# Third and fourth pass of a graph network: a quad's share of the fetching products moved ahead of the quad's own sums on TensorE

## The chip, the cores and the metric

The kernel runs on one core of one Trainium2 chip. The metric is the device time of one execution in microseconds (us), and of several executions the median. The core has a matrix engine (TensorE, PE in the profile, with PEld for its weight loads), a vector engine (VectorE, DVE), a scalar engine (ScalarE, ACT), GpSimd (POOL), and SyncE (SP), which here only issues transfers. GpSimd issues the gathers.

## The reference, cut to what matters

Four graph layers follow one another over 6250 nodes with 96 features and 106250 edges, which are sorted by target node. Each layer reads a row of a node table for each edge's source, and sums the rows (or takes their maximum) into the edge's target:

```
x = LN(x + attention layer(x))           # pass 1
x = LN(x + mean-and-max layer(x))        # pass 2, with a batch norm
# pass 3
msg = feat[src] * ci[src, None]
agg = segment_sum(msg, dst) * cj[:, None]
x = LN(x + (agg @ weight + bias))
# pass 4
msgs = (x @ W)[src] * edge_weight[:, None]
x = LN(x + LN(segment_sum(msgs, dst) + bias) * gamma + beta)
```

The change touches the sums `segment_sum` of passes 3 and 4 alone.

## The kernel before, in words

Edges are cut into tiles of 128, four tiles make a quad, four quads a group. There are 832 tiles and 208 quads in each of the four passes; `q` is the quad, `k = q % 4` its place in the ring of buffers.

**Gathers.** GpSimd runs through the quads (L630) and issues one indirect transfer for each tile of a quad, 128 rows of the node table into `rows[:, k, j]`. Before quad `q` it waits until the sums of quad `q - 4` are done, since these read the same buffer: `rows` is four quads deep.

**The sums of a quad.** VectorE writes `same` (L1348 in pass 3; L1696 in pass 4, times the edge's weight): a matrix of ones that says which of 128 target places an edge goes to. TensorE's `spread` (L728 through `window`) multiplies `rows` by `same`, four fp32 products that the profile counts as 8 matmuls. ScalarE adds the result to `acc` in its own `spread`: `part_sum` (L1028), a copy of 511 columns (L1030), one column with its carry (L1032). VectorE starts `same` of quad `q` when the sums of `q - 2` are done.

**Fetched tiles.** From quad 18 to quad 195 every third quad is picked (60 in each pass), and GpSimd gathers only three of its four tiles. The fourth comes from TensorE, out of a copy of the whole node table on the chip, split into three bf16 parts: 49 products of a one-hot matrix `found` with the table's 49 node tiles (L925), added up in `bank[0]`. They are cut into three pieces of 16, 16 and 17 products, which belong to the three quads ahead of the picked one: `piece(q)` gives the piece of quad `q`, and so every quad from 15 to 194 has one. VectorE's `find` writes the piece of `found` (L1588; ahead of a first piece also L1583), and after the third piece its `take` (L1595) adds the three parts of `bank[0]` up into `rows[:, k, 3]`. The order on VectorE within a quad is `same`, `take` if the quad is picked, `find`. TensorE's `spread` of a picked quad waits for `take`; its `fetch` waits for `find`.

**Side tiles.** In pass 3 the first 49 quads each carry one node tile more: ScalarE scales it into `x_two` (L1205), TensorE turns it (L950), ScalarE copies the result to `x_two_t` (L1209), TensorE multiplies it by `rhs_u` (L958), and ScalarE copies this to `xu` (L1215). ScalarE's order in a quad is L1205, L1209, then its `spread` with L1028, L1030 and L1032, then L1215:

```
wait(act, u_turned, q - 1)
act.activation(x_two[:, k % 2, :], tile_row(x_nodes, q), ACT.Identity, ...).then_inc(u_x, 1)
...
spread(q, k, acc, F, bank[2 + 2 * (k % 2)], part_sum, s2.agg_done, s2.held, s2.copied)
...
    wait(act, u_mm, q + 1)
    act.copy(tile_row(xu, q), bank[3][:, P:P + 2 * F]).then_inc(u_done, 1)
```

TensorE turns the tile of quad `q` only when `u_x` has counted `q + 1` and `u_done` has counted `q`. In pass 4 the first 49 quads also have a side tile, but on VectorE (L1705) and ScalarE (L1243) alone.

**The order on TensorE** within a quad of pass 3 is: turn (L950), [products of finished node tiles, L934, from quad 197 on], `spread`, product with `rhs_u` (L958), `fetch`. In pass 4 it is: [L934], `spread`, `fetch`. All engines take their instructions in the order of the program.

Of the kernel before, what the change touches and what calls it, by code (L numbers as in the profile page):

```python
# [38 lines left out]
def wait(eng, sem, value):  # L39
    if isinstance(value, int) and value <= 0:  # L40
        return
    if isinstance(sem, Signal):
        eng.wait_ge(sem.sem, value + sem.base)
    else:
        eng.wait_ge(sem, value)
# [27 lines left out]
def gnn_kernel(nc, N, E, dims, a):  # L73
# [18 lines left out]
    def tiles_of(c, n=NT):  # L92
        return range(c * CT, min(n, (c + 1) * CT))
# [8 lines left out]
    def ready(c):  # L102


        left = N - min(N, (c + 1) * CN)
        return -(-(E - left) // QE) - 1
# [11 lines left out]
    def piece(q):  # L118

        for m in range(EVERY):  # L120
            g = order_of.get(q + EVERY - m)
            if g is not None:
                return g, m
        return None
# [5 lines left out]
    def arrivals(n, q):  # L130

        return 16 * sum(gathers(m, p) for m in range(n + 1) for p in range(q % GQ, q + 1 if m == n else NQ, GQ))

    def ripe(slot, lag):

        return [c for c in range(NC) if ready(c) + lag == slot]

    ctx = ExitStack()
    with ctx:
# [114 lines left out]
        def exact(t, n=1):  # L254

            return near[:, t:t + n, :] if t < NEAR else far[:, t - NEAR:t - NEAR + n, :]
# [133 lines left out]
        def side_tile(q, kind):  # L390
            return kind and (not isinstance(q, int) or q < NT)

        def static(q):
            return isinstance(q, int)
# [275 lines left out]
        def _(pe):  # L670
# [47 lines left out]
            def group_offsets(i):  # L718

                _, at = nc.values_load_multi_w_load_instructions(offs[0:1, bass.ds(i * GQ * TQ, GQ * TQ)], engines=[pe.engine],  # L720
                                                                 min_val=0, max_val=QE - P, skip_runtime_bounds_check_because=NODES)
                return [at[k * TQ:(k + 1) * TQ] for k in range(GQ)]

            def window(out, nrow, at, left, right):

                for j in range(TQ):
                    here = bass.ds(at[j], P) if j else slice(0, P)
                    mm = pe.matmul(out[0:nrow, here], left(j), right(j), start=(j == 0), stop=(j == TQ - 1), skip_group_check=True)  # L728
                return mm
# [178 lines left out]
            def spread(s, q, i, k, at):  # L908

                wait(pe, s.same_done, q + 1)  # L910
                wait(pe, rows_in[k], arrivals(s.n, q))
                if q in order_of:
                    wait(pe, fetched, s.picks + order_of[q] + 1)
                wait(pe, s.copied, q - 1)
                window(bank[2 + 2 * (k % 2)], F, at, lambda j: rows[:, k, j, 0:F], lambda j: same[:, k % 2, j, :]).then_inc(s.agg_done.sem, 1)

            def fetch(s, q):

                at = piece(q)
                if at is None:  # L920
                    return
                g, m = at
                wait(pe, found_done, (s.picks + g) * EVERY + m + 1)
                for t in range(piece_of[m], piece_of[m + 1]):
                    mm = pe.matmul(bank[0][:, 0:PARTS * F], found[:, t, :], exact(t)[:, 0, :], start=(t == 0), stop=(t == NT - 1),  # L925
                                   skip_group_check=True)
                mm.then_inc(found_used.sem, 1)
# [3 lines left out]
            def products(c, nrow, rhs, freed, done):  # L931
                wait(pe, freed, c - 1)
                for m, t in enumerate(tiles_of(c)):
                    mm = pe.matmul(pair_of_banks[c % 2][m // 2][:, (m % 2) * 2 * F:(m % 2 + 1) * 2 * F], acc[0:nrow, t * P:(t + 1) * P],  # L934
                                   rhs[:], start=True, stop=True)
                mm.then_inc(done, 1)


            s2 = passes[2]
# [3 lines left out]
            def third_pass(i, kind):  # L943
                places = group_offsets(i)
                for k in range(GQ):
                    q = i * GQ + k
                    if side_tile(q, kind):
                        wait(pe, u_x, q + 1)
                        wait(pe, u_done, q)
                        pe.transpose(bank[3][0:F, 0:P], x_two[:, k % 2, :], ident[:]).then_inc(u_turned, 1)  # L950
                    if static(q):
                        for c in ripe(q, 1):
                            wait(pe, s2.copied, ready(c) + 1)
                            products(c, F, rhs_4, d_sum, d_mm)
                    spread(s2, q, i, k, places[k])
                    if side_tile(q, kind):
                        wait(pe, u_cols, q + 1)
                        pe.matmul(bank[3][:, P:P + 2 * F], x_two_t[:, k % 2, :], rhs_u[:], start=True, stop=True).then_inc(u_mm, 1)  # L958
                    fetch(s2, q)

            rolled(pe, third_pass, WITH_SIDE)
            for c in ripe(NQ, 1):
                wait(pe, s2.copied, ready(c) + 1)
# [3 lines left out]
            s3 = passes[3]  # L967
# [3 lines left out]
            def fourth_pass(i, kind):  # L971
                places = group_offsets(i)
                for k in range(GQ):
                    q = i * GQ + k
                    if static(q):
                        for c in ripe(q, 1):
                            wait(pe, s3.copied, ready(c) + 1)
                            products(c, F1, rhs_5, e_sum, e_mm)
                    spread(s3, q, i, k, places[k])
                    fetch(s3, q)  # L980

            rolled(pe, fourth_pass, PLAIN)
            for c in ripe(NQ, 1):
                wait(pe, s3.copied, ready(c) + 1)
# [794 lines left out]
```

## Time and profile before

| | |
|---|---|
| time, median of 3 runs (lowest, highest) | 4281.43 us (4277.96, 4282.35) |
| the profiled execution: its time, its span | 4278.2 us, 4276.2 us |
| busy: PE, DVE, ACT, POOL | 3037.4, 2905.5, 1377.3, 3094.2 us |
| pass 3, first to last gather issued | 2305.2 to 3268.8 us |
| pass 4, first to last gather issued | 3288.5 to 4254.8 us |
| mean granted clock of TensorE, as a share of full speed | 0.843 |

Busy time is summed over the span, so it says how full an engine is, not whether the others wait for it. In a timeline a row gives the start, the duration, the engine, the line, and in brackets how long the engine had been idle before it and what released it.

### The profile page before, as it was taken

To read this page: it belongs to the slowest core of one execution; us is meant where nothing else is said; L and a number is where in the kernel's file an instruction comes from. 1 tells how busy PE (TensorE), PEld (TensorE's weight loads), DVE (VectorE), ACT (ScalarE), POOL (GpSimd) and SP (SyncE) were. 2 spreads that over 40 slices of the span, in tenths; PEclk is the share of its full clock that TensorE was granted. 3 is DMA by queue.
4 is the path that set the end of the run, shared out by engine and by line. 5 is a ranking of instruction groups with operands and counts; after the bars stand their busy time and mean duration, and the time that the engine had idled before them with its cause. 6 is when DMAs were issued, how large, how long until landed. Compare 5 with 4: busy or idle time off the path is not lost.

```text
span 4276.2 us, 68563 instructions
## 1 busy us (share of the span) xinstructions
PE 3037.4 (71%) x20922; PEld 2603.9 (61%) x20922; DVE 2905.5 (68%) x5203; ACT 1377.3 (32%) x4318; POOL 3094.2 (72%) x3246
## 2 busy tenths in 40 slices
PE   7777777777666766676683787667775567776776
PEld 6677777777656666666662565555554455555555
DVE  4666666666676666666666566666665687777777
ACT  2222222222444444444454332222223222222223
POOL 5677777777277777777757777777776777777776
PEclk7777878777689888888895898999986699999997
DMA  7776776676443333333322222222222222222222
GB/s 216 202 188 178 188 187 182 182 188 179 105 121 100 100 98 100 100 100 98 100 74 62 49 45 45 45 45 45 45 44 67 55 45 44 45 45 46 44 45 56
DMA packets 363802, 417.49 MB, mean 98 GB/s; under 512 B 225184, under 2 KB 277011, under 8 KB 363357
## 3 DMA queue, kind: packets, MB, share of 16 engines
q0 software_dynamic: 129280, 239.67, 23.0%
q1 hardware_dynamic: 234173, 173.44, 15.2%
q8 instruction: 186, 3.05, 0.3%
q14 instruction: 163, 1.34, 0.1%
HBM read 393.05 MB, written 19.77 MB: 97 GB/s over the span
## 4 chain that ended last, share of the span: by engine, by line
POOL 61%; issue 21%; PE 8%; DMA 4%; DVE 3%; ACT 1%; SPq 1%; ACTq 0%; DVEq 0%; POOLq 0%
POOL rows L630 60%; PE bank L728 3%; DMA rows<-kv_table,src_idx 2%; DMA rows<-pair_table,src_idx 1%; PE bank L934 1%; POOL acc_max L657 1%; PE bank L825 1%; SPq L448 0%; PE bank L741 0%; PE bank L742 0%; PE bank L773 0%; PE bank L682 0%; DVE prod L1417 0%; DVE score L1419 0%; DVE prod L1415 0%
## 5 line engine op out<-in xcount | busy, mean ns | idle before, releaser
L728 PE MATMUL bank<-same,rows 128*96 128x128 f32 x4992 | 766.3, 304 | 364.8 <-issue 208.7
L630 POOL DMA_INDIRECT rows<-kv_table,src_idx x832 | 793.7, 954 | 314.1 <-issue 272.4
L630 POOL DMA_INDIRECT rows<-pair_table,src_idx x832 | 787.9, 947 | 311.5 <-issue 247.7
L728 PEld LDWEIGHTS bank<-same,rows 128*96 128x96 f32 x4992 | 658.7, 184 | 469.0 <-issue 407.8
L1030 ACT COPY acc<-bank 96x511 f32 (+1 forms) x832 | 480.1, 577 | 1365.8 <-PE bank L728 1364.6
L630 POOL DMA_INDIRECT rows<-h_table,src_idx x772 | 732.3, 949 | 253.7 <-issue 235.0
L630 POOL DMA_INDIRECT rows<-ci_table,src_idx x772 | 729.6, 945 | 243.3 <-issue 234.7
L1588 DVE TENSOR_TENSOR spare<-bank,first_only 128x2048 bf16<-128x2048 f32 x360 | 838.2, 2328 | 17.6
L925 PE MATMUL bank<-acc_max,spare 128*128 128x288 bf16 x4320 | 655.8, 307 | 164.8 <-DVE spare L1588 164.4
L925 PEld LDWEIGHTS bank<-acc_max,spare 128*128 128x128 bf16 x4320 | 437.6, 104 | 320.8 <-DVE spare L1588 194.1
L728 PE MATMUL bank<-same,msg 128*105 128x128 f32 x1664 | 307.6, 344 | 219.8 <-ACT acc L1032 219.5
L1348 DVE TENSOR_TENSOR same<-bank,rank_col 128x512 f32<-128x512 f32 x624 | 420.5, 674 | 41.8 <-PE bank L728 41.8
L741 PE MATMUL bank<-weights,first_only 97*128 97x96 f32 x1664 | 397.2, 329 | 33.3 <-DMA first_only<-q_table 29.6
L728 PEld LDWEIGHTS bank<-same,msg 128*105 128x105 f32 x1664 | 264.4, 225 | 239.8 <-DVE same L1348 174.1
L1487 DVE TENSOR_TENSOR_SCAN first_only<-first_only,bank 96x512 f32<-96x512 bf16 x208 | 264.7, 1273 | 199.4 <-issue 166.6
L742 PE MATMUL bank<-first_only 128*128 128x96 f32 x1664 | 399.0, 330 | 0.0
L825 PE MATMUL bank<-ident,rows 128*96 128x128 f32 x832 | 148.3, 307 | 305.9 <-DMA rows<-pair_table,src_idx 305.3
L741 PEld LDWEIGHTS bank<-weights,first_only 97*128 97x128 f32 x1664 | 335.1, 249 | 35.7 <-issue 35.6
L1595 DVE TENSOR_REDUCE rows<-bank 128x96 f32<-128x288 f32 x120 | 54.9, 457 | 430.2 <-PE bank L925 430.2
L742 PEld LDWEIGHTS bank<-first_only 128*128 128x128 f32 x1664 | 330.7, 246 | 0.0
L1415 DVE TENSOR_TENSOR prod<-bank,rows 128x384 f32<-128x384 f32 x208 | 115.6, 556 | 300.1 <-DMA rows<-kv_table,src_idx 235.1
L825 PEld LDWEIGHTS bank<-ident,rows 128*96 128x96 f32 x832 | 95.1, 138 | 346.1 <-DMA rows<-pair_table,src_idx 339.9
(184 smaller groups left out, 4172.6 us busy)
## 6 DMA issues: line engine op xcount, KB each, us to landing
first_only<-in_attr_cols SPq DMA_DIRECT2D x104, 384.0 KB, 4.1
first_only<-q_table SPq DMA_DIRECT2D x832, 48.0 KB
first_only<-rank_rows SPq DMA_DIRECT2D x104, 256.0 KB
first_only<-keep_rows SPq DMA_DIRECT2D x104, 192.0 KB, 3.2
rows<-kv_table,src_idx POOLq DMA_INDIRECT x832
rows<-pair_table,src_idx POOLq DMA_INDIRECT x832
rows<-ci_table,src_idx POOLq DMA_INDIRECT x772
rows<-h_table,src_idx POOLq DMA_INDIRECT x772
```

What stands on the lines that cost most here:

```text
L630: pool.indirect_dma_start(rows[:, k, j, 0:width], None, table, bass.IndirectOffsetOnAxis(ap=src_idx[:, t:t + 1], axis=0)).then_inc(rows_in ...
L728: mm = pe.matmul(out[0:nrow, here], left(j), right(j), start=(j == 0), stop=(j == TQ - 1), skip_group_check=True)
L741: pe.matmul(quad(bank[k % 2], F)[:, j, :], attr[:, k, j * P:(j + 1) * P], w_e, start=True, stop=True)
L742: mm = pe.matmul(quad(bank[2 + k % 2], F)[:, j, :], pick[:, k % 2, j * P:(j + 1) * P], q_win[:, k, j, :], start=True, stop=True)
L825: tr = pe.transpose(bank[k % 2][0:F, j * P:(j + 1) * P], rows[:, k, j, F:PAIR], ident[:])
L925: mm = pe.matmul(bank[0][:, 0:PARTS * F], found[:, t, :], exact(t)[:, 0, :], start=(t == 0), stop=(t == NT - 1), skip_group_check=True)
L1030: act.copy(dst[0:nrow, bass.ds(first + 1, QE - 1)], src[0:nrow, 1:QE])
L1348: return dve.tensor_tensor(out, base, over(values[:, bass.ds(q * TQ, TQ)], n), ALU.is_equal)
L1415: dve.tensor_tensor(prod[:], quad(bank[2 + k % 2], F), rows[:, k, :, 0:F], ALU.mult).then_inc(prod_step, 1)
L1487: dve.tensor_tensor_scan(scanned[:, k % 2, :], keep_row[:, k, :], bank[k % 2][0:F, :], 0.0 if static(q) and q == 0 else scanned[:, (k - 1) ...
L1588: dve.tensor_tensor(found[:, lo:hi, :], away.rearrange("p (o e) -> p o e", o=1).to_broadcast([P, hi - lo, P]), over(hundreds[:, lo:hi], P) ...
L1595: dve.tensor_reduce(rows[:, k, TQ - 1, 0:F], bank[0][:, 0:PARTS * F].rearrange("p (m f) -> p f m", m=PARTS), AX_X, ALU.add).then_inc(fetch ...
```

## The change

TensorE's `fetch` of a quad is called before its `spread` of the same quad in both passes. Nothing else changes: the instructions, their number, their waits and what the other engines do are the same.

```diff
@@ third_pass
                             products(c, F, rhs_4, d_sum, d_mm)
+                    fetch(s2, q)
                     spread(s2, q, i, k, places[k])
                     if side_tile(q, kind):
                         wait(pe, u_cols, q + 1)
                         pe.matmul(bank[3][:, P:P + 2 * F], x_two_t[:, k % 2, :], rhs_u[:], start=True, stop=True).then_inc(u_mm, 1)
-                    fetch(s2, q)
@@ fourth_pass
                             products(c, F1, rhs_5, e_sum, e_mm)
+                    fetch(s3, q)
                     spread(s3, q, i, k, places[k])
-                    fetch(s3, q)
```

## Rows read from the trace of the kernel before

**Rows 1.** The page: the chain that ended last, by engine.
```profile
POOL 61%; issue 21%; PE 8%; DMA 4%; DVE 3%; ACT 1%; SPq 1%; ACTq 0%; DVEq 0%; POOLq 0%
```
**Rows 2.** Waits of POOL from 2300 to 4276 us: total, times, longest.
```profile
POOL rows L630 <- issue: 469.6, 1541, 0.3
...
POOL rows L630 <- PE bank L728: 0.3, 1, 0.3
```
**Rows 3.** The tile `rows`: duration ns min/median/max, first and last start.
```profile
L630 POOL DMA_INDIRECT rows<-ci_table,src_idx x772: 940/944/1292, 2305.2 to 3268.8; - x193
L630 POOL DMA_INDIRECT rows<-h_table,src_idx x772: 940/944/1302, 3288.5 to 4254.8; - x193
```
**Rows 4.** Timeline of pass 3, quads 23 to 25, all engines but POOL.
```profile
2426.22 0.65 PE L925 MATMUL bank<-acc_max,spare 128*128 128x288 bf16 x4
...
2428.50 0.46 DVE L1595 TENSOR_REDUCE rows<-bank 128x96 f32<-128x288 f32 x1 [4.26 <-PE bank L925]
...
2429.21 1.08 PE L728 MATMUL bank<-same,rows 128*96 128x128 f32 x8 [0.64 <-DVE rows L1595]
...
2429.37 2.29 DVE L1588 TENSOR_TENSOR spare<-bank,first_only 128x2048 bf16<-128x2048 f32 x1
...
2430.13 0.49 PE L958 MATMUL bank<-rhs_u,acc_max 97*128 97x192 f32 x2
2430.42 0.58 ACT L1030 COPY acc<-bank 96x511 f32 x1 [1.10 <-PE bank L728]
...
2431.25 0.48 ACT L1205 ACTIVATE acc_max<-x_nodes,s_all,r_all 128x96 f32<-128x96 f32 x1
...
2431.72 2.13 PE L925 MATMUL bank<-acc_max,spare 128*128 128x288 bf16 x16 [1.09 <-DVE spare L1588]
...
2433.69 0.27 PE L950 MATMUL bank<-ident,acc_max 128*96 128x128 f32 x1
...
2433.80 1.06 PE L728 MATMUL bank<-same,rows 128*96 128x128 f32 x8
```
**Rows 5.** Timeline of pass 3 at TensorE's half clock; quads 12, 13, 15, 51.
```profile
2372.54 1.99 PE L728 MATMUL bank<-same,rows 128*96 128x128 f32 x8 [1.07 <-issue]
...
2374.66 0.58 ACT L1030 COPY acc<-bank 96x511 f32 x1 [2.44 <-PE bank L728]
...
2376.02 0.45 PE L950 MATMUL bank<-ident,acc_max 128*96 128x128 f32 x1 [0.84 <-DMA rows<-ci_table,src_idx]
...
2387.44 0.45 PE L950 MATMUL bank<-ident,acc_max 128*96 128x128 f32 x1 [0.85 <-DMA rows<-ci_table,src_idx]
...
2390.03 2.82 PE L925 MATMUL bank<-acc_max,spare 128*128 128x288 bf16 x16
...
2555.05 3.81 PE L925 MATMUL bank<-acc_max,spare 128*128 128x288 bf16 x16 [1.32 <-DVE spare L1588]
```
**Rows 6.** Timeline of pass 3: quads 18 and 48, and quad 52's first gather.
```profile
2402.99 0.58 ACT L1030 COPY acc<-bank 96x511 f32 x1 [1.10 <-PE bank L728]
...
2540.37 0.58 ACT L1030 COPY acc<-bank 96x511 f32 x1 [1.10 <-PE bank L728]
...
2551.07 0.94 POOL L630 DMA_INDIRECT rows<-ci_table,src_idx  x1 [0.30 <-issue]
```
**Rows 7.** Timeline of pass 4: take of a picked quad, find two quads on.
```profile
3467.64 0.46 DVE L1595 TENSOR_REDUCE rows<-bank 128x96 f32<-128x288 f32 x1 [2.33 <-PE bank L925]
...
3475.41 2.41 DVE L1588 TENSOR_TENSOR spare<-bank,first_only 128x2176 bf16<-128x2176 f32 x1
```
**Rows 8.** Windows: busy us (instructions) of PE, PEld, DVE, ACT, POOL; PE clock, DMA.
```profile
2401.00:2541.00 140.00, 111.62 (x832) 88.34 (x830) 95.71 (x83) 57.15 (x184) 105.72 (x112) 0.96 0.23 45
2541.00:3275.00 734.00, 536.16 (x3761) 413.26 (x3761) 492.69 (x555) 175.06 (x523) 550.99 (x584) 0.92 0.22 47
...
3380.00:3527.00 147.00, 105.53 (x777) 79.56 (x775) 117.79 (x208) 41.81 (x126) 111.10 (x118) 0.97 0.21 45
3527.00:4201.00 674.00, 495.81 (x3571) 376.17 (x3569) 521.46 (x836) 152.53 (x443) 509.76 (x539) 0.94 0.21 45
```

## The prediction

> **What bounds the kernel now.** I read the page's chain first. GpSimd's gathers and "issue", which is the gap between one gather and the next, hold 82% of it; PE holds 8% [rows 1]. So I asked next whether GpSimd ever waits in passes 3 and 4. In 1976 us it waits for TensorE once, for 0.3 us; all else is the fixed gap of 0.3 us after each gather [rows 2]. Each pass then is 772 gathers at one rhythm: (3268.8 - 2305.2) / 771 = 1.250 us in pass 3, (4254.8 - 3288.5) / 771 = 1.253 us in pass 4 [rows 3]. Three quads with one picked hold 11 gathers, 13.75 us, and whatever the other engines do inside that is free as long as GpSimd is never made to wait.
>
> GpSimd would wait if the sums of quad q - 4 came late. How late they may come I read from one quad: the result of quad 48 is copied from 2540.37 on, the first gather of quad 52 starts at 2551.07 [rows 6]. That is 10.7 us; with 0.1 us for the signal, 10.6 us. This is the cover of everything that the change does, and the question is whether a delay of the sums can add up to more.
>
> **What the change moves.** Nothing is removed or added. In pass 3 and pass 4, 180 pieces each (60 picked quads, three pieces) move ahead of the sums of their own quad. TensorE still alternates piece, sums, piece, sums; the piece between the sums of quads q - 1 and q is now that of q and not that of q - 1. No transfer is issued by TensorE, so no queue is passed. Behind the moved piece stand the sums of the quad (and so ScalarE's addition and, four quads on, the gathers), and in pass 3 the product with the side tile. Two waits change places.
>
> *First, the picked quad.* Before, the last piece ran after the sums of the quad ahead of it, and VectorE stood idle 4.26 us until `take` could start [rows 4]. Now that piece runs earlier, while TensorE would have waited for rows. This is a gain of latency, worth nothing in time: the sums of a picked quad already come 10.6 us before anyone needs them.
>
> *Second, the side tiles of pass 3, quads 15 to 48.* After the sums of a quad ScalarE has a run of work that ends with `x_two` of the next quad: 2430.42 to 2431.25 + 0.48 = 2431.73 [rows 4]. TensorE may turn the next side tile only then. Before, the piece was computed during this run and hid it. Now the piece stands behind the turn, so that TensorE idles during ScalarE's run, and the run and the piece add up. The closed loop for one quad, sums to sums:
> - start of the sums to ScalarE's copy: 2430.42 - 2429.21 = 1.21 us [rows 4]
> - copy to the next turn: 1.36 us (2374.66 to 2376.02, where TensorE had been idle) [rows 5]
> - turn to the next product: 2433.80 - 2433.69 = 0.11 us [rows 4]
> - a piece of 16 to what follows it: 2433.69 - 2431.72 = 1.97 us [rows 4]
>
> The sum is 4.65 us. For the first piece of a picked quad another path is longer: last piece of the quad ahead, `take`, `find`, first piece, which takes 2431.72 - 2426.22 = 5.50 us [rows 4]; it is made of the same waits in both kernels. Three quads: 5.50 + 2 x 4.65 = 14.80 us against GpSimd's 13.75. The delay of the sums grows by 1.05 us for every three quads.
>
> *How late it starts.* Quad 15 is the first with a piece, at TensorE's half clock (a turn takes 0.45 us, [rows 5], and not 0.27, [rows 4]). Its piece now starts right after the turn at 2387.44, at about 2387.7. In the trace of before the clock rises within this piece at about 2391.6: it takes 2.82 us, between 2.13 at full and 3.81 at half clock [rows 4, 5]. So the new piece is slow throughout, 1.97 x 3.81 / 2.13 = 3.5 us to the sums at 2391.2. If the rest is at full clock: copy 2392.4, next piece 2393.9, then 2398.5, then quad 18's first piece 2404.0, its sums 2406.0, copy 2407.2. Before it was 2402.99 [rows 6]: 4.2 us late. Bounds: 2.7 us if the clock is up already in quad 15; with two more quads at half clock 9.2 us, since such a loop is (2374.66 - 2372.54) + 1.36 + 0.22 + 3.5 = 7.2 us and not 4.65 [rows 5].
>
> *What comes out.* Quad 48 is ten threes after quad 18: 4.2 + 10 x 1.05 = 14.7 us late, with a cover of 10.6. GpSimd stalls about 4.1 us in total, in small pieces from about quad 42 on. With the starting bounds it is 2.6 to 9.1 us; 0.05 us more or less in each loop moves it by 1.5. From quad 49 on the turn is gone and TensorE catches up in a few quads. What GpSimd lost stays lost, since it is the bound to the end of the pass.
>
> *Elsewhere in the two passes* I cost the change at nothing. Pass 4 is the tighter: from `take` to the third piece's `find` end it is 3475.41 + 2.41 - 3467.64 = 10.2 us [rows 7], then a last piece with its signal, 2428.50 - 2426.22 = 2.3 us [rows 4], 12.5 us a round against 13.75. ScalarE's side work there doesn't involve TensorE. If this cover went (every product at half clock), TensorE's two pieces and one quad of sums in that round would add about 4.5 us, 3.2 more than it has room for. The mean clock of these stretches is 0.92 to 0.97 [rows 8], so a round like that stays alone and the 10.6 us take it. The change has nothing after quad 194, so the ends of the passes stay.
>
> Sum: 4278.2 us (profiled execution) + 4.1 = 4282.3. The median of the runs lies 3.2 us above that execution, so I add the 4.1 to it: 4285.5. A measurement of this kernel can tell about 0.2% from no change, 8.6 us; 4.1 us is under it.
>
> **Rivals.**
> *A. The cover holds.* If the loop is 0.15 us shorter than I add up, or quad 15 begins at full clock, the delay stays under 10.6 us and nothing is seen: 4281.4. For it: GpSimd has never waited so far [rows 2]. Against it: each term of the loop is a row, and the round of 14.80 has to be read wrong by 0.4 us.
> *B. The other side: TensorE's clock falls in the side quads.* Mean granted clock is 0.96 there now, with TensorE busy 111.6 of 140 us, 80%; right after it, busy 73% (536.2 of 734), it is 0.92 [rows 8]. Clock and business go together, and the change brings business down to about 11.0 us in 14.8, 74%, with TensorE idle twice in a row at each picked quad (about 1.1 us before the turn and 0.7 after it). A fall costs what a slow piece costs, 3.81 - 2.13 = 1.7 us [rows 4, 5], now on the loop. Eleven picked quads with one fall each: 18.5 us, 4304. From three falls on (4.1 + 5.1 = 9.2 us) it is slower by more than 0.2%; half of the eleven gives 4295.
> The Trainium skill, TensorE: Matmul & The Clock Gate, section "HAM oscillation — how this bites in real kernels", tells of a kernel whose matmuls waited for data in each tile, and whose clock fell again in every single one. By that rule it is a fall for every picked quad, 4304 us. The trace of before agrees only in part: TensorE idled in each of these quads too, and the clock averaged 0.96.
> *C. The clock stays down* through all 34 side quads: 34 x (7.2 - 13.75 / 3) - 10.6 = 78 us, 4360. Against it: at half clock TensorE is nearly always busy in this loop, and the clock rose under just such work at quad 15.
> *D. Faster.* The earlier `take` could only help if something waited for the sums; no row shows that. What remains is a better clock at the ends of the passes: about 4270.
>
> **Chances.** Forecast, a stall of 1 to 8.6 us: 0.49; A 0.17; B 0.27; C, or the round of pass 4 turning into the bound, 0.03; D 0.04. Within 0.2% are the forecast and A, 0.66; slower B and C, 0.30; faster 0.04. The predicted time is the likeliest case's, 4285.5 us, its own range 4282.5 to 4290. The range of 8 in 10 takes in A with the scatter of the runs below and most of B above: 4279 to 4299; outside are the worst of B, C and D.
>
> **What the profile after would show.** GpSimd in pass 3 waits for the sums (L728) some microseconds in total, all within the quads just before and after 48, and not in pass 4; the distance from the copy of a quad to the first gather four quads on shrinks from 10.7 us at quad 18 to nearly nothing at 48, and is back before quad 75. In quads 15 to 48 the turn follows the copy of the quad before by 1.36 us every time, with TensorE idle ahead of it, and the picked quads are 14.8 us apart. VectorE's idle time ahead of `take` falls. Wrong I am if the turn doesn't wait for ScalarE, if the round there is below 13.75 us, if the clock of 2401 to 2541 us falls under 0.9, or if GpSimd waits for TensorE in the rest of the passes.

## The result, and the profile after

| | before | after |
|---|---|---|
| time, median (lowest, highest) of 7 runs | 4281.10 us (4277.68, 4284.53) | 4295.52 us (4290.71, 4302.98) |
| the profiled execution: time, span | 4278.2, 4276.2 us | 4290.71, 4288.7 us |
| first to last gather of pass 3 | 963.6 us | 979.1 us |
| first to last gather of pass 4 | 966.3 us | 967.0 us |
| granted clock, quads 18 to 48 of pass 3 | 0.96 | 0.93 |

The ratio is 1.0036, 95% interval 1.0026 to 1.0046: 14.4 us slower, by more than the 0.2% that such a measurement tells from no change. The whole of it lies in pass 3 (979.1 - 963.6 = 15.5 us). In the profiled execution the work ahead of pass 3 took 3.2 us less than in the one of before, which has nothing to do with the change, and so its span grew by 12.5 us alone.

The page of the kernel after, chain by engine; the waits of GpSimd in pass 3 (2301.5 to 3281.1 us); its gathers (min/median/max ns, first and last start):

```profile
POOL 31%; PE 29%; DVE 16%; issue 15%; DMA 5%; ACT 2%; SPq 1%; ACTq 0%; DVEq 0%; POOLq 0%
```
```profile
POOL rows L630 <- issue: 230.4, 756, 0.3
POOL rows L630 <- PE bank L728: 20.4, 14, 3.0
```
```profile
L630 POOL DMA_INDIRECT rows<-ci_table,src_idx x772: 938/944/1281, 2302.0 to 3281.1; - x193
L630 POOL DMA_INDIRECT rows<-h_table,src_idx x772: 940/944/1166, 3299.8 to 4266.8; - x193
```

Against [rows 1] the chain has moved from GpSimd to PE, VectorE and, in small part, ScalarE. That alone must not be read as a loss: a chain passes through whatever released the last instruction, and a kernel below that loses nothing has PE and DVE in it as well. The waits say it. Before, GpSimd never waited for the sums (L728) beyond its usual gap [rows 2]; now it does 14 times, up to 3.0 us. Six of these are just the gap of 0.30 us. The other eight are these gathers (timeline, all of them):

```profile
2451.65 0.94 POOL L630 DMA_INDIRECT rows<-ci_table,src_idx  x1 [0.85 <-PE bank L728]
...
2468.10 0.94 POOL L630 DMA_INDIRECT rows<-ci_table,src_idx  x1 [3.01 <-PE bank L728]
...
2563.36 0.94 POOL L630 DMA_INDIRECT rows<-ci_table,src_idx  x1 [3.03 <-PE bank L728]
```

The five between have 2.93, 1.36, 3.03, 1.35 and 3.04 us. With the gap taken off, the eight come to 18.6 - 8 x 0.3 = 16.2 us, close to the 15.5 us of the pass; the rest is scatter. They are the first gathers of quads 31, 34, ... 52, and each waits for the sums of a picked quad, 27, 30, ... 48.

Now the loop, in the quads that answer to [rows 4] (timeline, all engines but GpSimd; quads 24 to 27):

```profile
2436.72 0.58 ACT L1030 COPY acc<-bank 96x511 f32 x1 [4.63 <-PE bank L728]
...
2441.36 0.58 ACT L1030 COPY acc<-bank 96x511 f32 x1 [2.21 <-PE bank L728]
...
2442.19 0.47 ACT L1205 ACTIVATE acc_max<-x_nodes,s_all,r_all 128x96 f32<-128x96 f32 x1
...
2442.72 0.31 PE L950 MATMUL bank<-ident,acc_max 128*96 128x128 f32 x1 [1.16 <-ACT acc_max L1205]
...
2442.87 0.65 PE L925 MATMUL bank<-acc_max,spare 128*128 128x288 bf16 x4
...
2444.95 1.04 PE L728 MATMUL bank<-same,rows 128*96 128x128 f32 x8
2445.15 0.46 DVE L1595 TENSOR_REDUCE rows<-bank 128x96 f32<-128x288 f32 x1 [3.19 <-PE bank L925]
...
2446.11 0.58 ACT L1030 COPY acc<-bank 96x511 f32 x1 [2.33 <-PE bank L728]
...
2448.37 2.13 PE L925 MATMUL bank<-acc_max,spare 128*128 128x288 bf16 x16 [0.58 <-DVE spare L1588]
...
2451.50 0.58 ACT L1030 COPY acc<-bank 96x511 f32 x1 [2.96 <-PE bank L728]
```

The copy of quad 25 starts at 2441.36, `x_two` of quad 26 is done at 2442.66, and the turn starts at 2442.72, after 1.16 us in which TensorE had nothing to do; it names ScalarE as what released it. Only then come the piece and the sums. The row of `x_two` is the same work as in [rows 4]; what is new is that the piece no longer covers it. From copy to copy it is 4.64, 4.75 and 5.39 us, 14.78 us for three quads (2451.50 - 2436.72), and GpSimd needs 13.75. At 2451.65, 0.15 us after the copy of quad 27 has begun, the first gather of quad 31 starts: where there were 10.7 us between such rows [rows 6], nothing is left.

The next three quads take longer, 16.45 us from 2451.50 on, and so do seven of the ten rounds between quad 18 and quad 48. The three from 21 to 24 show why (timeline, quad 24):

```profile
2431.03 0.32 PE L950 MATMUL bank<-ident,acc_max 128*96 128x128 f32 x1 [1.16 <-ACT acc_max L1205]
...
2431.92 2.99 PE L925 MATMUL bank<-acc_max,spare 128*128 128x288 bf16 x16 [0.58 <-DVE spare L1588]
...
2434.70 1.90 PE L728 MATMUL bank<-same,rows 128*96 128x128 f32 x8
```

The piece took 2.99 us and not 2.13, the sums 1.90 and not 1.04: the granted clock had gone from 2.4 to 1.2 GHz in them, after TensorE had been idle for 1.16 us, turned one tile, and been idle for 0.58 us again. The window over them gives a mean clock of 0.63 (busy us of PE, PEld, DVE, ACT, POOL; clock, the third number from the end):

```profile
2432.00:2436.60 4.60, 4.60 (x26) 3.85 (x26) 2.66 (x2) 0.08 (x1) 3.38 (x5) 0.63 0.19 39
```

I call this a fall of the clock. It costs 16.45 - 14.78 = 1.67 us each time (1.57 us once). The falls are in the first pieces of quads 21, 24, 30, 33, 39, 45 and 48. In quads 27, 36 and 42 TensorE has the same two idle stretches, 1.16 and 0.58 us, and the clock stays up.

### The profile page after: what moved, and what is told of

Read it like the earlier page. It is cut to its first block, busy times and chain, and to the rows that moved or that the text cites. A ratio compares the mean times of both kernels' runs of the same rounds, so it can differ in the third digit from the quotient of the medians.

```text
span 4288.7 us, 68563 instructions
## 1 busy us (share of the span) xinstructions
PE 3060.4 (71%) x20922; PEld 2624.1 (61%) x20922; DVE 2921.4 (68%) x5203; ACT 1375.8 (32%) x4318; POOL 3094.9 (72%) x3246
## 4 chain that ended last, share of the span: by engine, by line
POOL 31%; PE 29%; DVE 16%; issue 15%; DMA 5%; ACT 2%; SPq 1%; ACTq 0%; DVEq 0%; POOLq 0%
POOL rows L630 30%; PE bank L925 15%; PE bank L728 8%; DVE spare L1588 8%; DMA rows<-kv_table,src_idx 2%; DMA rows<-pair_table,src_idx 1%; DVE same L1696 1%; DVE rows L1595 1%; PE bank L934 1%; PE bank L741 1%; PE bank L742 1%; DVE bank L1583 1%; DVE prod L1417 1%; DVE score L1419 1%; DVE prod L1415 1%
## 5 line engine op out<-in xcount | busy, mean ns | idle before, releaser
L728 PE MATMUL bank<-same,rows 128*96 128x128 f32 x4992 | 763.1, 303 | 338.3 <-issue 301.6
L728 PEld LDWEIGHTS bank<-same,rows 128*96 128x96 f32 x4992 | 665.4, 185 | 421.6 <-issue 409.8
L925 PE MATMUL bank<-acc_max,spare 128*128 128x288 bf16 x4320 | 677.3, 314 | 152.8 <-DVE spare L1588 140.3
L728 PE MATMUL bank<-same,msg 128*105 128x128 f32 x1664 | 312.6, 348 | 212.4 <-ACT acc L1032 212.2
L728 PEld LDWEIGHTS bank<-same,msg 128*105 128x105 f32 x1664 | 268.9, 228 | 233.1 <-DVE same L1348 183.5
L1696 DVE TENSOR_SCALAR same<-iota_s,rank_col,src_hi 128x128 f32<-128x128 f32 x832 | 233.2, 358 | 125.5 <-PE bank L728 125.0
```

What stands on the lines that cost most here:

```text
L1696: ins = dve.tensor_scalar(same[:, k % 2, j, :], iota_s[:], rank_col[:, at], weight_col[:, at], ALU.is_equal, ALU.mult)
```

## The experiments

All times are medians, each beside the kernel before on the same chip. The chips differed much more than the kernels: on two of them the kernel before took 4279.6 and 4278.8 us, as above, on three others 5142, 5152 and 5237 us.

**1. The changed kernel once more.**

> The changed kernel itself once more, on the chip of the experiments. On the chips of the seven kernels run so far the kernel before took 5142 to 5152 us and not 4281, and a round of three quads in pass 3 took GpSimd about 16.5 us and not 13.75. My theory: against rounds that long a loop of 14.8 us (16.45 with a fall of the clock) can't make the sums late, and the change makes no difference there, ratio 1.000 within 0.002. If this chip gives 4281 us for the kernel before, the loss of 14.4 us is back. Rival (the change costs a fixed time wherever it runs): ratio 1.003 on either.

This chip gave 4279.63 us for the kernel before, and 4293.77 us for the change: ratio 1.0031 (1.0019 to 1.0044). The loss is back, of the same size. The gathers of pass 3 took 978.8 us (979.1 in the first profile), and GpSimd waited for the sums 10 times in it, 18.2 us in all. Six of the ten rounds between quads 18 and 48 have a fall of the clock here (16.35 or 16.45 us), and so has quad 18 ahead of them, whose copy is 4.75 us late. On such a chip the theory and its rival expect the same, so this run repeats the loss and doesn't part the two.

**2. The piece ahead of the turn.** In pass 3 the order is now piece, turn, sums, product; pass 4 is as in the changed kernel. The piece is still ahead of the quad's sums everywhere.

```diff
                     q = i * GQ + k
+                    fetch(s2, q)
                     if side_tile(q, kind):
                         wait(pe, u_x, q + 1)
...
-                    fetch(s2, q)
                     spread(s2, q, i, k, places[k])
```

> The same kernel as in the run of the order piece, turn, sums, now hoped for on a chip that gives about 4280 us for the kernel before. My theory: the piece lies in ScalarE's run again, the round of three quads is 13.75 us, GpSimd never waits for the sums for more than its usual gap, ratio 1.000 (within 0.001). Rival (a piece ahead of the sums costs by itself): the ratio stays at 1.003.

4276.59 us against 4278.81, ratio 0.9996 (0.9987 to 1.0005): the loss is gone, and nothing is gained. The waits of GpSimd in pass 3, its gathers, a window over quads 18 to 48 (busy us of PE, PEld, DVE, ACT, POOL; clock), and the timeline:

```profile
POOL rows L630 <- issue: 235.0, 771, 0.3
```
```profile
L630 POOL DMA_INDIRECT rows<-ci_table,src_idx x772: 940/944/1287, 2301.2 to 3264.4; - x193
```
```profile
2397.00:2546.20 149.20, 115.58 (x891) 91.63 (x889) 103.84 (x89) 59.56 (x192) 112.91 (x120) 1.00 0.23 45
```
```profile
2449.14 0.58 ACT L1030 COPY acc<-bank 96x511 f32 x1 [1.90 <-PE bank L728]
...
2449.64 2.13 PE L925 MATMUL bank<-acc_max,spare 128*128 128x288 bf16 x16 [0.30 <-DVE spare L1588]
...
2449.97 0.48 ACT L1205 ACTIVATE acc_max<-x_nodes,s_all,r_all 128x96 f32<-128x96 f32 x1
...
2451.61 0.27 PE L951 MATMUL bank<-ident,acc_max 128*96 128x128 f32 x1
```

All 771 of these waits are the gap, the pass takes 963.2 us, and the piece begins 0.50 us after the copy and lies over ScalarE's run. `x_two` is ready at 2450.45, ahead of the turn at 2451.61. A piece ahead of the sums costs nothing that could be measured, in neither pass; a piece behind the turn does. This also answers where in the two passes the loss is, since here all 360 pieces are moved. The page of this kernel gives PE 15% and DVE 10% of its chain, and yet it is as fast as the one of before.

**3. The idle time filled.** The changed kernel with three products more in each of the quads 15 to 48 of pass 3, whose results nobody uses:

```diff
                         pe.matmul(bank[3][:, P:P + 2 * F], x_two_t[:, k % 2, :], rhs_u[:], start=True, stop=True).then_inc(u_mm, 1)
+                        if q >= 15:
+                            for _ in range(3):
+                                pe.matmul(bank[5][:, 0:P], ident[:], iota_s[:], start=True, stop=True)
```

> The same kernel as in the run with three unused products in each of the quads 15 to 48, now hoped for on a chip that gives about 4280 us for the kernel before. Theory of the clock: granted clock near 1.00 in these quads and not 0.92, every round 14.8 us, GpSimd loses 3.8 us, ratio 1.0009 (1.000 to 1.0015). Rival (the rounds of 16.45 us come from the order or a late find): ratio 1.003 or more, clock whatever it is.

4281.79 us against 4278.81, ratio 1.0002 (0.9993 to 1.0011). By the medians it is 3.0 us slower than its own kernel before, which the interval doesn't tell from nothing (its upper end is 4.7 us); the change alone was slower by 14.4 and 14.1 us. So with more work the loss is about 11 us smaller. A window over quads 18 to 48; GpSimd's waits and gathers in pass 3; the timeline:

```profile
2403.10:2552.30 149.20, 128.75 (x1015) 109.59 (x1014) 96.28 (x83) 56.25 (x181) 109.83 (x117) 1.00 0.21 44
```
```profile
POOL rows L630 <- PE bank L728: 8.4, 11, 1.4
```
```profile
L630 POOL DMA_INDIRECT rows<-ci_table,src_idx x772: 938/944/1289, 2307.3 to 3275.3; - x193
```
```profile
2492.91 0.58 ACT L1033 COPY acc<-bank 96x511 f32 x1 [2.33 <-PE bank L728]
2492.95 0.83 PE L962 MATMUL bank<-iota_s,ident 128*128 128x128 f32 x6
...
2494.27 0.32 PE L950 MATMUL bank<-ident,acc_max 128*96 128x128 f32 x1 [0.49 <-ACT acc_max L1208]
```

The fill (L962) takes 0.83 us of the idle time and leaves 0.49; the turn still comes 1.36 us after the copy. The granted clock is 1.00, and every one of the ten rounds is 14.77 or 14.78 us. GpSimd's gathers took 968.0 us: 4.4 us over the 963.6 of before. By the sum of the prediction with this run's start (quad 18's copy 4.6 us late): 4.6 + 10 x 1.03 - 10.6 = 4.3 us. So the change has two costs, and this run parts them: the loop itself some 4 us, the falls of the clock the other 11 (979.1 - 968.0 = 11.1 us between the gathers). The order on TensorE and the wait for `find` (0.58 us) are those of the changed kernel, so neither is what made its long rounds.

**4. On the three other chips.** Nine runs fell on them. One pass changed alone:

```diff
# pass 4 as before, pass 3 as changed (third_only); or the other way round (fourth_only)
-                    fetch(s3, q)
                     spread(s3, q, i, k, places[k])
+                    fetch(s3, q)
```

> The change in pass 3 alone; pass 4 keeps the order of before. My theory (the side-tile loop of pass 3 is the whole cost): the full loss of 14.4 us stays, about 4295 us (4290 to 4300), ratio 1.0034, and GpSimd waits for the sums some 15 us, all between quads 27 and 53. Rival (the moved piece costs in each pass, through the clock or VectorE): about half of it, 4288.

> The change in pass 4 alone; pass 3 keeps the order of before. My theory: no difference, 4281 us, ratio 1.000 within 0.001, and no wait of GpSimd for the sums. Rival (cost in each pass): about 4288.

The pieces moved in some quads of pass 3 alone (`q < 24` or `q < 36`, pass 4 as before; `q >= NT`, which is 49, with pass 4 changed):

```diff
-                    fetch(s2, q)
+                    if q < 36:
+                        fetch(s2, q)
                     spread(s2, q, i, k, places[k])
...
+                    if not (q < 36):
+                        fetch(s2, q)
```

> In pass 3 the piece goes ahead of the sums in quads 15 to 23 alone, then behind them as before; pass 4 as before. Theory of the cover: late by 4.0 us at quad 18 and by 1.04 us (2.7 with a fall of the clock) more for each of two rounds, 6 to 9.4 us, under 10.6: no time lost, 4281 us, GpSimd never waits. Rival (each moved quad costs its share of the loss): 9 of 34 quads, 3.8 us, 4285.

> The same for quads 15 to 35. Theory of the cover: six rounds, 4.0 + 6 x (1.04 to 2.7) less 10.6, with a fall in seven of ten rounds 6.6 us lost (0 to 9.6), 4288 us; GpSimd waits in quads 30 to 40 and no later. Rival (each quad its share): 21 of 34, 8.9 us, 4290, and waits spread over all the changed quads.

> In pass 3 the piece goes ahead of the sums only from quad 49 on, where no side tile is; pass 4 as in the changed kernel. So 146 of 180 pieces of pass 3 and all of pass 4 are moved. My theory: no difference, 4281 us, ratio 1.000, no wait of GpSimd for the sums. Rival (moved pieces cost everywhere): 4290 or more.

The last two again:

> The same kernel as in the run with the pieces moved in quads 15 to 35 of pass 3 alone, now hoped for on a chip that gives about 4280 us for the kernel before. Theory of the cover: by quad 36 the sums are late by 4.0 us and six rounds of 1.04 us (no fall) to 2.7 (a fall in each), less the cover of 10.6: 0 to 9.6 us lost, with a fall in seven of ten rounds 6.6 us, ratio 1.0015; GpSimd's waits for the sums lie between quads 30 and 42 and none is ahead of them. Rival (each moved quad its share): 21 of 34, 8.9 us, waits from quad 19 on.

> The same kernel as in the run with the pieces moved from quad 49 of pass 3 on and in all of pass 4 (326 of 360 pieces), now hoped for on a chip that gives about 4280 us for the kernel before. My theory: ratio 1.000 (within 0.001), GpSimd waits for the sums in neither pass beyond its usual gap. Rival (moved pieces cost everywhere): nine tenths of the loss, 1.003.

| run | before | this | ratio (95%) |
|---|---|---|---|
| pass 3 alone | 5142 | 5156 | 1.0017 (0.9992 to 1.0042) |
| pass 4 alone | 5142 | 5151 | 1.0015 (0.9992 to 1.0039) |
| piece, turn, sums | 5142 | 5147 | 1.0001 (0.9978 to 1.0025) |
| idle time filled | 5142 | 5143 | 0.9995 (0.9967 to 1.0024) |
| quads 15 to 23 | 5152 | 5149 | 0.9987 (0.9963 to 1.0010) |
| quads 15 to 35 | 5152 | 5158 | 1.0011 (0.9992 to 1.0031) |
| quads 15 to 35, again | 5237 | 5242 | 1.0015 (0.9998 to 1.0032) |
| from quad 49 on | 5152 | 5136 | 0.9975 (0.9949 to 1.0001) |
| from quad 49 on, again | 5237 | 5260 | 1.0041 (1.0023 to 1.0059) |

The third and the fourth are the kernels of experiments 2 and 3, with these expectations:

> Both passes changed, but in pass 3 the piece goes ahead of the turn of the side tile too, so that it lies in ScalarE's run again. My theory (the piece behind the turn adds to ScalarE's run): the round of three quads is 13.75 us again, GpSimd never waits, 4281 us, ratio 1.000. Rival (a piece ahead of the sums costs by itself, since it delays them by 2 us and find comes late): the loss stays at 4290 to 4295.

> The changed kernel with three fp32 products of 128 columns more in each quad from 15 to 48 of pass 3, put behind the product with the side tile, results unused: they fill some 0.8 us of the 1.16 us in which TensorE idles for ScalarE. Theory of the clock: the falls in these quads go, every round of three is 14.8 us, late by 4.0 + 10 x 1.04 at quad 48, less the cover of 10.6: 3.8 us lost, 4285 us, although TensorE does more work. Rival (the longer rounds of 16.45 us come from the order itself or a late find): still 4295, or worse by the filler's own time.

These runs decide nothing. The kernel before alone scattered from 5115 to 5178 us beside the first four, and eight of the nine intervals hold 1. The profiles show another machine (timeline of the kernel with pass 3 alone, pass 3):

```profile
2973.87 1.04 PE L728 MATMUL bank<-same,rows 128*96 128x128 f32 x8
...
2976.70 0.46 DVE L1595 TENSOR_REDUCE rows<-bank 128x96 f32<-128x288 f32 x1 [6.33 <-remote]
2976.88 0.58 ACT L1030 COPY acc<-bank 96x511 f32 x1 [4.18 <-remote]
2977.03 0.94 POOL L630 DMA_INDIRECT rows<-ci_table,src_idx  x1 [2.06 <-remote]
```

The sums end at 2974.91; ScalarE's copy, which follows them by 0.12 us in the rows of the changed kernel, starts 1.97 us later, and VectorE and GpSimd start at nearly the same time, all after waits that the profile puts down to "remote". The idle times in the brackets also hold what the engine would have waited without that. GpSimd alone has 231 such waits in this execution, 433.5 us, 4.1 us at most, and pass 3 took 1170 us here from the first gather to the last. GpSimd also waits for the sums on such a chip where pass 3 is as before: in the kernel with pass 4 changed alone 24 times in pass 3, 68.8 us, and 27 times, 91.7 us, in this one. So the premise that it never waits doesn't hold there, and single executions that scatter by tens of microseconds don't tell these two apart. The rival of experiment 1, a fixed cost wherever the kernel runs, can't be excluded from such numbers; nor do they show that the change is free there. The kernel with the pieces moved from quad 49 on has come out on both sides, 0.9975 and 1.0041, with intervals that exclude each other. Why, stays open. On a chip of the first kind it wasn't run; there experiment 2, with the same pieces moved and all others too, stands at 0.9996.

## Why the prediction was right and wrong

**Right: where and by what.** The forecast put the only cost into the side tiles of pass 3, quads 15 to 48, through TensorE's turn behind ScalarE's run. Experiment 2 takes just this away and the loss with it. Copy to turn was to be 1.36 us and is 1.36; a round was to be 14.80 us and is 14.78 wherever the clock holds. Quad 18 was to be 4.2 us late and was 4.05 (2403.82 - 2301.97 against 2402.99 - 2305.19 us after the first gather; 4.75 in the repeat).

**Right: the cover.** Quads 15 to 26 moved the sums late without a single wait of GpSimd. The first wait comes with quad 31's gather, when quad 27's copy is 10.5 us late. At quad 48 they were 26.1 us late (261.24 us after the first gather, 235.18 before): 26.1 - 10.6 = 15.5 us, and the pass took 15.5 us longer. That the loss is what is left of the lateness after the cover is shown by this profile and by the filled one (4.3 by the sum, 4.4 measured); the runs that were to cut it short at quads 23 and 35 fell on the other chips and add nothing.

**Wrong: the clock, and with it the case.** The step that failed is "if the rest is at full clock", and the term is the number of falls in the ten rounds: I took none, there were seven of 1.67 us. Lateness at quad 48 was to be 14.7 us; with 7 x 1.67 = 11.7 it is 26.4, measured 26.1. This is rival B, to which I gave 0.27, with the price of one fall (1.7 us) and its place (the two idle stretches at a picked quad, 1.1 and 0.7 us; measured 1.16 and 0.58) as it came. That its typical time, 4295 us, meets the measured 4295.5 so closely is in part luck: it stood for five and a half falls, and with seven the same sum gives 4297.

I weighed B too low because the mean clock in these quads was 0.96 in spite of idle time in each of them. That mean hid what it was made of. In the trace of before the clock is 1.00 up to quad 38, and then it falls three times (timeline of the kernel before, the piece behind quad 39's sums; two windows):

```profile
2500.51 3.80 PE L925 MATMUL bank<-acc_max,spare 128*128 128x288 bf16 x16 [1.09 <-DVE spare L1588]
...
2505.41 0.58 ACT L1030 COPY acc<-bank 96x511 f32 x1 [0.25 <-PE bank L728]
```
```profile
2401.00:2499.00 98.00, 75.24 (x585) 60.40 (x584) 66.87 (x59) 39.73 (x128) 74.00 (x79) 1.00 0.22 45
2499.00:2541.00 42.00, 36.39 (x249) 27.95 (x248) 28.83 (x25) 17.42 (x56) 31.72 (x34) 0.88 0.23 46
```

The pieces behind quads 39, 42 and 45 took 3.8 us each and not 2.13. They made the copies of quads 40, 43 and 46 1.7 us later, which left 9.5 us to the gathers and not 11.2, and each was made up within its round; so they cost nothing. Counted into the loop of the forecast, these three alone give 14.7 + 3 x 1.67 - 10.6 = 9.1 us, about 4290.5 us. The falls weren't new; with the change there were seven and not three, and they stood in a loop that was already too long.

What decides whether the clock falls in a round stays open. Shown is only that filling most of the first idle stretch ends the falls. Two idle stretches with nothing but a turn between them can't be needed, since before they were 0.64 and 1.09 us, with sums and a product between them [rows 4]; and they aren't enough, since three rounds of the changed kernel have them and no fall. The busy share doesn't tell it either, against what rival B assumed: before it was 80% at a clock of 0.96, in experiment 2 it is 77% (115.58 of 149.20 us) at 1.00.

The prediction also leaned on the Trainium skill, TensorE: Matmul & The Clock Gate, section "HAM oscillation — how this bites in real kernels", for a fall at every picked quad. The kernel on that page waits some 3 to 5 us for data in each tile, and the longest idle stretch at a picked quad of the changed kernel is 1.16 us, so its falls don't carry over to this case by themselves. The trace has a fall in seven rounds of ten. Experiment 3 shows that the falls end when idle time is filled, by 1.00 against 0.93 in the window and ten rounds without a fall.

**Wrong in consequence: where the waits are.** They were to lie around quad 48; with the falls the cover was gone by quad 27. The distance from copy to gather was to be back before quad 75; at quad 78 it was still 7.9 us, and it was full again only at quad 84.

**Right: elsewhere nothing.** In pass 4 GpSimd waited for the sums for no more than its gap (six times 0.3 us after quad 48 of pass 3 and six in pass 4), and its gathers took 967.0 us against 966.3. VectorE's idle time ahead of `take` fell from 4.26 to 3.19 us, and nobody gained by it.

Rival A fell with the first wait, C with the clock, which was back within a quad after each fall. The range of 4279 to 4299 held the time. The chance of "slower by over 0.2%" was put at 0.30, and it is what happened.

## What to carry to other kernels

Before moving a block of work on one engine, ask what other engine's latency it covers where it stands: here a piece of 2 us hid the 1.36 us of ScalarE's run, and one call put behind or ahead of the turn made the difference. Where a buffer ring gives cover, add up the lateness over all iterations, since a loop that is 7% too long (14.78 us against 13.75) eats any ring in the end, and only what is beyond the ring costs time. And don't read a mean clock of 0.96 as "no falls": look for the slow rows in it. A fall that costs nothing while the work behind it has time to spare costs its full 1.67 us once that work is on the path.

## What the runs showed of the hardware that I had not expected

TensorE's clock fell in seven of ten rounds in which it was busy 111.0 of 149.2 us, and in none of ten with 0.83 us of unused products in the first idle stretch of each quad; the unused work was worth 11 us. In the kernel before it fell three times in the same quads, each time behind idle stretches of 0.64 and about 1.1 us, and nobody waited for it. The same kernel took 4279 us on two chips and 5142 to 5237 us on three others, where ScalarE, VectorE and GpSimd sit through waits together that end by "remote", on GpSimd 231 of them with 433.5 us in one execution.
